# Order of transfers and of softplus work at the start of a scan stage, in a fused decoder layer on one core

## The reference

```python
x = x + mamba(_layernorm(x), ...)           # part 1
x = x + quantized_mlp(_layernorm(x), ...)   # part 2: int8 gate/up and down, its own weights per batch
x = x + moe(_layernorm(x), ...)             # part 3: 16 experts, top 2, and a shared expert
```

```python
delta = softplus(dt_proj(dt) + dt_bias)     # (512, 1024)
h = h * exp(delta * A) + (delta * u) * B_t  # over t = 0..511
y = sum over states of h * C_t
y = (y + u * D) * silu(z);  out_proj(y)
```

## Time and profile before

| | |
|---|---|
| time, median of 3 runs | 1636.22 us (1634.85 to 1637.94) |
| profiled execution, its own time | 1631.51 us |
| its span in the profile | 1629.8 us |
| TensorE busy | 1406.2 us, 86% |
| VectorE busy | 1323.2 us, 81% |
| GpSimd busy | 1036.9 us, 64% |
| ScalarE busy | 799.3 us, 49% |
| chain that ended last, by engine | PE 30%, DVE 17%, issue 11%, POOL 9%, ACT 3%, DMA 1% |

### The profile page before, as it was taken

One profiled execution on the slowest core, in us unless ns is written; L12 is line 12 of the kernel. 1 busy time (PEld: TensorE's weight loads), 2 busy tenths in 40 slices (PEclk: granted clock), 3 DMA queues, 4 the chain that ended last, 5 costly groups with the idle time before them and its releaser, 6 DMA issues.

```text
span 1629.8 us, 19427 instructions
## 1 busy us (share of the span) xinstructions
PE 1406.2 (86%) x5462; PEld 817.8 (50%) x5462; DVE 1323.2 (81%) x2196; ACT 799.3 (49%) x1365; POOL 1036.9 (64%) x672
## 2 busy tenths in 40 slices
PE   7597678999899899999899899999899999647994
PEld 4333223444555565444665565444555664336783
DVE  4589999688899999798899999798899999773212
ACT  3676444257544765247545765247545664131131
POOL 0299999103999898403999898403999898323001
PEclk9889899999899999999899999999899999868997
DMA  3550000413536783614537682614546783601984
GB/s 119 230 194 26 1 0 1 168 52 131 190 133 217 212 244 104 220 46 160 191 129 225 214 242 97 218 46 163 194 137 196 220 242 103 228 26 53 349 332 138
DMA packets 94074, 252.14 MB, mean 155 GB/s; under 512 B 11024, under 2 KB 11152, under 8 KB 88848
## 3 DMA queue, kind: packets, MB, share of 16 engines
q1 hardware_dynamic: 86688, 229.93, 42.0%
q0 software_dynamic: 5120, 16.78, 3.1%
q10 hardware_dynamic: 2160, 4.19, 0.8%
HBM read 207.87 MB, written 42.99 MB: 154 GB/s over the span
## 4 chain that ended last, share of the span: by engine, by line
PE 30%; DVE 17%; issue 11%; POOL 9%; ACT 3%; DMA 1%; DVEq 0%; POOLq 0%; ACTq 0%; SPq 0%
PE bank L1994 7%; DVE bank L1309 5%; POOL work L688 4%; PE bank L1836 3%; PE bank L2120 3%; PE bank L2023 3%; PE bank L1931 2%; PE bank L1926 2%; PE bank L1920 2%; PE bank L1970 2%; DVE work L1319 1%; PE bank L2015 1%; DVE pairs L1319 1%; POOL xs_dram L771 1%; DVE rr L1493 1%
## 5 line engine op out<-in xcount | busy, mean ns | idle before, releaser
L688 POOL TENSOR_TENSOR work<-du,BB 128x1024 f32<-128x1024 f32 x255 | 600.6, 2367 | 5.0 <-DVE work L1580 3.5
L980 ACT ACTIVATE bank<-delta,A_sb 128x512 f32<-128x512 f32 x512 | 349.2, 690 | 443.0 <-DVE pairs L1319 249.6
L1309 DVE TENSOR_TENSOR_SCAN bank<-bank,work 128x512 f32<-128x512 f32 x432 | 522.7, 1220 | 30.1 <-ACT bank L980 16.7
L1994 PEld LDWEIGHTS bank<-x3T,ew_up 128*128 128x128 f32 x1488 | 221.4, 196 | 80.2 <-issue 59.4
L1994 PE MATMUL bank<-x3T,ew_up 128*128 128x128 f32 (+1 forms) x1488 | 244.3, 311 | 11.3 <-DMA ew_up<-in_exp_w 9.1
L1319 DVE TENSOR_TENSOR pairs<-bank,CB 128x512 f32<-128x512 f32 x240 | 160.9, 670 | 3.0 <-PE bank L1931 2.5
L1319 DVE TENSOR_TENSOR work<-bank,CB 128x512 f32<-128x512 f32 x192 | 128.4, 669 | 0.0
L1926 PE MATMUL bank<-pairs,ident 128*128 128x512 f32 x160 | 89.2, 641 | 42.3 <-POOL pairs L741 17.8
L640 POOL TENSOR_TENSOR col<-col,halfpow 128x4 f32<-128x4 f32 (+1 forms) x8 | 7.8, 973 | 175.3 <-DVE col L1457 175.3
L2120 PE MATMUL bank<-wst,zg 128*128 128x512 f32 x256 | 117.0, 593 | 0.8 <-issue 0.8
L1849 PE MATMUL bank<-xT,wst 128*128 128x512 f32 x256 | 115.2, 597 | 0.0
(11 more groups left out here) (261 smaller groups left out, 2362.9 us busy)
## 6 DMA issues: line engine op xcount, KB each, us to landing
ew_up<-in_exp_w SPq DMA_DIRECT2D x93, 512.0 KB
ew_dn<-in_exp_w SPq DMA_DIRECT2D x93, 256.0 KB
hm<-xs_dram SPq DMA_DIRECT2D x69, 256.0 KB, 4.5
ys_dram<-x3T SPq DMA_DIRECT2D x69, 256.0 KB, 4.6
wst<-in_w_in SPq DMA_DIRECT2D x64, 256.0 KB, 2.6
BB<-bc_dram SPq DMA_DIRECT2D x16, 1024.0 KB, 4.8
CB<-bc_dram SPq DMA_DIRECT2D x16, 1024.0 KB, 6.9
wst<-in_out_w SPq DMA_DIRECT2D x32, 256.0 KB, 2.7
```

The lines of the kernel that those rows point to most:

```text
L688: nc.gpsimd.tensor_tensor(dBu[:, k % CHUNK_SLOTS, :, :], du[:, j % 2:j % 2 + 1, :].broadcast_to([P, 2, T]), BB[:, n0:n0 + 2, :], ALU.mult) ...
L980: nc.scalar.activation(R[q % RING][:, :], delta[:, j, :], ACT.Exp, scale=A_sb[:, j, n:n + 1]).then_inc(S["da_ready"], 1)
L1309: V.tensor_tensor_scan(prod[c % (2 * PAIR_SLOTS)] if on_pool(q) else R[q % RING][:, :], R[q % RING][:, :], dBu[:, c // 2 % CHUNK_SLOTS, c ...
L1994: ins = mm(gu_bank(v)[:, part * n:(part + 1) * n], w[:, part * D + k * P:part * D + (k + 1) * P], rhs, start=(k == 0), stop=(k == KD - 1))
```

## The change

Three pieces of the order are changed; no instruction is added or removed.

```diff
+LOGS_AT = 2
...
                     weights("o", b, 0, 4)
+                    load_first_experts(b - 1)
                     wait(sp, "linkO", 3 * TT * b)
                     broadcasts(b, 2)
-                    load_first_experts(b - 1)
                     broadcasts(b, 3)
                     load_experts(b - 1)
...
-                        if k == 3 and b > 0:
+                        if k == 4 and b > 0:
                             for i in range(4, 8):
                                 softplus_sum(b, i)
-                        if k == 4 and b > 0:
+                        if k == 5 and b > 0:
                             for i in range(4, 8):
                                 softplus_less(b, i)
...
                             for i in range(KD if scan else KD // 2):
                                 x3(i)
-                            if scan:
-                                lns(b, range(4, 8))
                     if scan and b > 0:
+                        if p == LOGS_AT:
+                            lns(b, range(4, 8))
                         for m in SILU_AT.get(p, ()):
                             z_silu(b, m)
```

## The result

The changed kernel is slower: median 1648.8 us (1645.7 to 1653.2) against 1638.4 us (1634.8 to 1642.5) of the kernel before, nine runs of each on the same chips. The ratio is 1.0068, 95% interval 1.0052 to 1.0083, that is 11.1 us (8.5 to 13.6) on 1638.4. The forecast was 7.7 us slower, 1643.9 us, from a base of 1636.2.

The account below looks back on a forecast made before the run. GpSimd was taken to bound the first 75 us of a stage, to chunk 17; its new standing of 2.0 + 3.3 + 2.4 = 7.7 us on a 1636.22 us median gave 1643.9 us, range 1636.5 to 1650.0.

Parts of the forecast that it names:

- Pacemaker and cover: First 75 us of stages 1 to 3: GpSimd sets the pace; sums put behind chunk 4 no longer cover its broadcast.
- The weights in the same queue: Before chunk 4: 1.835 MB ahead of group 2 delays its C half 4.5 to 4.6 us; GpSimd stands 7.7 us total.
- The estimate that the prediction made of it: Chunk 4, by 2.0 us plus bytes over 436 GB/s: GpSimd stands 1.0 us a stage, 3 us in all.
- The logarithms: ScalarE: VectorE's 3.5 us wait for unit 3 goes, most returns at unit 5's decay, ending at 1153.5; cost zero.
- TensorE "behind nothing" that VectorE waits for: After removal of TensorE's 3.1 us wait for first expert weights: worth nothing, as neither GpSimd nor VectorE waits for TensorE there.
- A (no standing): Broadcast group 2 shares the engines with the weights, not queued behind: standing 1.8 us in all, 1638.0 us; chance 0.13.
- B (VectorE last): VectorE last at chunk 17; earlier chunk 5 removes its 1.7 us wait a stage, 5.1 in all: 1631.1 us; chance 0.08.
- C (the C half of group 3 late): Group 3's C half takes 8.3 us; unit 12's product stands 2.3 us a stage, 6.9 in all: 1649.5 us; chance 0.12.

Follow-up runs that it names:

- the one attempt to relieve VectorE in turn: Against the kernel with VectorE's sums through PSUM: logarithms moved behind unit 3's decay, sums ahead of unit 4's scan; 1626.6 us, ratio 0.9932 to the kernel before.

## Why the prediction was right, and where not

**Pacemaker and cover: right.** GpSimd sets the time to chunk 17 (relieved of its sums it shortened the stretch by 12.0 us, made to stand again it gave 8.8 back), and the sums had been the cover of the third broadcast, group 2 (transfer order alone, transfer order put back).

**The weights in the same queue: right in kind, too small in size.** The term was 2.0 + 3.3 + 2.4 = 7.7 us of standing; it measured 3.7 + 3.8 + 3.0 = 10.5. GpSimd was ready where the prediction had it, 8.6 us after chunk 1, so the whole error is in the landing of the C half. Counted from the issue of the first transfer it was put at 12.0, 13.3 and 12.4 us and took 13.7, 13.8 and 12.9. Windows of the changed kernel in stage 1 (columns as in the earlier trace rows):

```profile
413.00:416.00 3.00, 1.97 (x16) 1.73 (x16) 2.97 (x3) 2.86 (x6) 2.92 (x3) 1.00 0.72 235
416.00:424.00 8.00, 7.90 (x44) 7.12 (x45) 6.99 (x9) 6.57 (x12) 7.07 (x4) 0.79 1.01 398
424.00:425.00 1.00, 1.00 (x6) 0.86 (x5) 0.00 (x0) 1.00 (x1) 0.00 (x0) 0.97 0.71 295
425.00:426.00 1.00, 1.00 (x4) 0.49 (x3) 0.19 (x1) 0.99 (x3) 0.00 (x0) 1.00 0.06 25
```

and the first three microseconds of the same place in the kernel before:

```profile
410.63:413.63 3.00, 1.97 (x16) 1.73 (x16) 2.97 (x3) 2.86 (x6) 2.92 (x3) 1.00 0.83 281
```

With the weights in front the queue starts slower, 235 against 281 GB/s over three microseconds, 0.14 MB or 0.3 us behind, and then runs at 398 where 411 was assumed, 0.3 us over the rest. That is about the 0.5 us that stages 2 and 3 were short. In stage 1 another microsecond comes at the end. The bytes run out near 425, but 25 GB/s still flow up to 426. The trace has the 16 counts by which a transfer raises its semaphore: fifteen of the C half had come by 425.7 us and the last came at 426.7, 0.9 us behind. In stage 1 of the kernel before the last was 0.1 us behind the fifteenth (418.0 and 418.1). In stage 2 of the kernel before it was 1.1 us behind (784.0 and 785.2), which is why the C half took 8.3 us there and why the forecast for stage 2 came nearer. So one late part of the transfer comes with and without the weights ahead; why it comes in some stages and not in others is open.

The Trainium skill's page "DMA: Bandwidth & Descriptors", section "Anatomy of one DMA — SWDGE (gpsimd) path", gives its sum for one transfer that GpSimd issues, while these seven were issued by SyncE one behind the other. The estimate that the prediction made of it, 1.0 us of standing a stage, is further off than the rows: by it the queue would have taken 11.0 us from the first issue to the last landing, and it took 13.7, 13.8 and 12.9.

**The logarithms: right in the times.** The decay of unit 5 was put at 11.4 us behind chunk 1 (1153.5 - 1142.11) and came there (its scan starts at 1164.88, and 1164.88 - 1153.47 = 11.4). Put back, they change no time that can be told; what they do to the stretch stands below.

**TensorE "behind nothing" that VectorE waits for: not so.** The prediction put this at nothing. In the changed kernel VectorE waits 2.6, 2.6 and 2.4 us for TensorE's sum of block 0 (0.2 us before) and 2.1, 1.8 and 1.6 us for a tanh behind TensorE (no such wait before). TensorE in turn stands 1.6 us for the pair of units 6 and 7, which GpSimd starts 27.3 us behind chunk 1 in place of 24.3 (1166.40 - 1142.11), and 1.5 us for GpSimd's product after it (1.6 before). Its granted clock lies at 0.50, the level of 1.2 GHz, from 1175 to 1187 us; before it fell, TensorE had stood 3.1 us for values of the routing (hm) from VectorE (1.7 before). Windows of 11 us, 27 us behind chunk 1, changed kernel, before, and with the transfer order put back:

```profile
1180.47:1191.47 11.00, 7.88 (x14) 3.51 (x15) 9.06 (x18) 3.07 (x5) 11.00 (x8) 0.63 0.36 144
```

```profile
1169.11:1180.11 11.00, 9.40 (x30) 5.35 (x29) 10.90 (x21) 3.32 (x6) 10.26 (x10) 1.00 0.25 82
```

```profile
1173.13:1184.13 11.00, 8.80 (x26) 5.36 (x26) 10.10 (x19) 3.76 (x6) 10.26 (x10) 0.84 0.44 162
```

A granted clock of 0.63 against 1.00 is a mixture of the levels of 1.2 and 2.4 GHz, and 14 matmuls stand in the window where there were 30. The third row has no stand and a clock of 0.84: its stretch is 0.9 us longer than before, and the other two stages of that kernel, at 0.92 and 1.00, are not longer.

What these waits cost is open. The stretches grew by 13.0 us and the standing is 10.5, so at most 2.5 us are theirs. Against them speaks the version with the logarithms put back: it has the same waits of VectorE and a clock of 0.66 in the same window, and its stretches grew by no more than its standing (11.6 and 11.5). What it lacks is the wait for the decay of unit 5. So the late logarithms, harmless while GpSimd doesn't stand, may have a share in the 2.5 us; no run separates the two, and the two times (+9.3 and +11.1 us) can't be told apart.

**Rivals.** A (no standing) is refuted by the gap and by its growth with the bytes. B (VectorE last) is refuted for this kernel; with GpSimd relieved of its sums VectorE is close to it, but the one attempt to relieve VectorE in turn showed no difference. C (the C half of group 3 late) did not occur: no wait for it stands in VectorE's lists.

**The number.** In total the time grew by 11.1 us (8.5 to 13.6). The terms above, 7.7 forecast, 2.8 of standing that was missed and 2.5 of the rest, add up to the 13.0 us of the profiled stretches, which the interval of the time includes. The measured 1648.8 us lies 4.9 over the forecast and 1.2 under the upper end of its range. Of the 4.9 us, 2.2 are the base: the kernel before took 1638.4 us beside the changed one, where 1636.2 was assumed. The range reached up to 1650.0 for the sake of rival C, which did not occur, so that the measured time lies inside it is in part luck.

## What to carry to other kernels

Two reorderings that each show no cost alone can cost together, when one takes away the work behind which the other's transfer was hidden; before moving work on the engine that sets the pace, ask what lands under it. Order the transfers of one queue by what the pacing engine waits for, and count the bytes ahead. A wait that is seen on an engine which is not the pacemaker (here TensorE's 3.1 and VectorE's 3.5 us) buys nothing when removed; the idle time is better used to take work off the pacemaker, which gave 9 us here.

## What the runs showed of the hardware

A VectorE sum of 128 x 512 took 0.69 us with one input in PSUM and 2.12 us (mean of twelve) with both in SBUF beside a busy GpSimd, and beside such sums a GpSimd pair took 1.71 us in place of 1.27 and a chunk 2.79 in place of 2.36. Moving one operand to PSUM turned 8 us slower into 9 us faster.

The last of the 16 counts of a 1 MB transfer came 0.1 to 1.1 us behind the fifteenth, in a queue that moved about 400 GB/s (418.0 and 418.1 us, 784.0 and 785.2 in the kernel before; 425.7 and 426.7 in the changed one). The engine that waits for it stands for this last count, though nearly all of the data are there.
